# Half a tile of logits, one expert's first products and one addition take other places in a transformer layer's instruction streams

## What is computed

```python
q = einsum(layernorm(x), Wq) / 8;  k = einsum(ctx, Wk);  v = einsum(ctx, Wv)
attn = einsum('bqhd,bkhd->bhqk', q, k)
attn = softmax(einsum('bhqk,hi->biqk', attn, Wth1))
attn = einsum('bhqk,hi->biqk', attn, Wth2)
x = x + einsum(einsum('bhqk,bkhd->bqhd', attn, v), Wo)
feat = layernorm(x).reshape(2048, 256)
scores = layernorm(feat, g, b) @ centroids.T
for e in range(8):            # balanced: each expert takes its 256 best of the rows left
    idx = top_k(where(taken, -inf, scores[:, e]), 256); taken[idx] = True
routed = feat[all idx].reshape(8, 256, 256)
h = gelu(layernorm(routed, g, b) @ w1[e] + b1[e]) @ w2[e] + b2[e]
x = x + (routed + h, put back in row order)
```

## Time and profile before

| | us |
|---|---|
| median of 3 runs | 310.98 (310.86 to 312.36) |
| the profiled execution, its own time | 311.05 |
| span in its profile | 309.3 |
| PE busy in the span | 291.3 |
| DVE busy | 229.2 |
| POOL busy | 198.8 |
| ACT busy | 151.0 |
| device memory read and written | 37.46 MB, mean 121 GB/s |

### The profile page before, as it was taken

One profiled execution on the slowest core, in us unless ns is written; L12 is line 12 of the kernel. 1 busy time (PEld: TensorE's weight loads), 2 busy tenths in 40 slices (PEclk: granted clock), 3 DMA queues, 4 the chain that ended last, 5 costly groups with the idle time before them and its releaser, 6 DMA issues.

```text
span 309.3 us, 6795 instructions
## 1 busy us (share of the span) xinstructions
PE 291.3 (94%) x2151; PEld 252.6 (82%) x2151; DVE 229.2 (74%) x799; ACT 151.0 (49%) x275; POOL 198.8 (64%) x248
## 2 busy tenths in 40 slices
PE   7999998999999999999987779999999999999990
PEld 3989997999999999999982239797989898989980
DVE  0569999888887888888877877777777777338750
ACT  1257646355555555554546424544444454564720
POOL 8200333467888888877742785949787878768841
PEclk9999999999999999999999999999999999999996
DMA  7995002971000000000116420555656565712120
GB/s 254 359 368 207 3 0 76 368 271 35 36 34 34 34 34 34 34 34 35 37 67 206 135 70 2 157 187 166 214 170 208 175 206 174 222 37 69 36 74 28
DMA packets 21769, 37.79 MB, mean 122 GB/s; under 512 B 2416, under 2 KB 14960, under 8 KB 21360
## 3 DMA queue, kind: packets, MB, share of 16 engines
q1 hardware_dynamic: 19184, 31.16, 29.4%
q0 software_dynamic: 2560, 6.31, 6.7%
HBM read 31.17 MB, written 6.29 MB: 121 GB/s over the span
## 4 chain that ended last, share of the span: by engine, by line
PE 77%; DVE 11%; issue 3%; POOL 3%; DMA 2%; ACT 1%; POOLq 0%; DVEq 0%
PE pair L1208 68%; PE pair L1284 4%; PE pair L1258 2%; DVE cmpb L1018 2%; PE pair L1452 1%; PE pair L1296 1%; DMA G<-rows_scratch,idx 1%; DMA out_dram<-G,idx 1%; DVE sm L875 1%; DVE wneg L789 1%; DVE pair L1052 1%; DVE hp L1140 1%; POOL out_dram L543 1%; DVE ok L1035 1%; POOL pr L284 0%
## 5 line engine op out<-in xcount | busy, mean ns | idle before, releaser
L1208 PE MATMUL pair<-yT,w1p 128*128 128x256 f32 x384 | 53.3, 290 | 0.0
L1208 PE MATMUL pair<-Bm,pT 128*128 (+1 forms) x384 | 50.4, 287 | 0.2 <-ACT pT L630 0.2
L1208 PEld LDWEIGHTS pair<-yT,w1p 128*128 128x128 f32 x384 | 48.2, 191 | 0.5 <-POOL yT L528 0.2
L1208 PE MATMUL pair<-Am,xTp 128*128 (+1 forms) x192 | 48.3, 400 | 0.0
L1208 PEld LDWEIGHTS pair<-Bm,pT 128*128 128x128 f32 x384 | 47.1, 191 | 0.4 <-issue 0.4
L1208 PE MATMUL pair<-w2s,hT 128*128 128x256 f32 x192 | 47.1, 389 | 0.0
L284 POOL TENSOR_TENSOR pr<-pr,rs 128x1024 f32<-128x1024 f32 (+1 forms) x16 | 31.3, 1955 | 24.3 <-DVE rs L882 15.2
L522 POOL TENSOR_TENSOR w1p<-w1s,w1p 128x512 fp32r<-128x512 f32 x32 | 40.1, 1280 | 5.7 <-ACT w1p L696 5.6
L1208 PEld LDWEIGHTS pair<-Am,xTp 128*128 128x128 f32 x192 | 34.9, 188 | 6.9
L1208 PEld LDWEIGHTS pair<-w2s,hT 128*128 128x128 f32 x192 | 33.8, 190 | 4.3
L741 ACT ACTIVATE hT<-pair,b1s 128x256 f32<-128x256 f32 x48 | 20.2, 471 | 34.4 <-PE pair L1208 20.9
(11 more groups left out here) (156 smaller groups left out, 573.6 us busy)
## 6 DMA issues: line engine op xcount, KB each, us to landing
w1s<-w_dram SPq DMA_DIRECT2D x8, 1024.0 KB
w2s<-w_dram SPq DMA_DIRECT2D x7, 1024.0 KB, 5.8
rows_scratch<-row SPq DMA_DIRECT2D x16, 256.0 KB, 2.0
xs<-x_dram SPq DMA_DIRECT2D x1, 2048.0 KB, 16.7
xTs<-xT_dram SPq DMA_DIRECT2D x1, 2048.0 KB, 18.4
wk_s<-wk_dram SPq DMA_DIRECT2D x1, 1024.0 KB, 5.5
wv_s<-wv_dram SPq DMA_DIRECT2D x1, 1024.0 KB, 7.6
wqT_s<-wqT_dram SPq DMA_DIRECT2D x2, 512.0 KB, 9.2
```

What stands on the lines that cost most here:

```text
L1208: return nc.tensor.matmul(out_, l, r, start=start, stop=stop)
```

## The change

1. Attention: the statistics of tiles 8 to 15 and their variances leave the fills and come at the end of VectorE's steps 2, 3 and 4; the second root follows in GpSimd's step 5 instead of 0, ACT's wait for it in step 6 instead of 4, and steps 5 and 6 are now written out ahead of the loop. TensorE's step 2 makes the first half (bank) of tile 2's logits ahead of the transposition of tile 0.
2. First expert: in slot 1 its rounded products for f = 0 stand ahead of round 7's total, f = 2's rounded products and the rests of both ahead of the ranks, f = 1 behind the ranks and f = 3 behind the spreading; five filler matmuls go. Slot 2 gets tables of its own for expert 0, with `tokens` and `spread` one piece earlier, and expert 1's first product ahead of the ranks. For all experts ACT's copies come in the order yT(0), yT(1), yF(0), yF(1); the rest of expert 0's second half is made by VectorE ahead of `select(1)`.
3. Last expert: `final(6, 1)` stands ahead of the two `hidden_split` calls of slot 9.

```diff
-        A_FIRST, A_LOOP, A_LOOP_END, A_LAST = -1, 5, 15, T + 4
+        A_FIRST, A_LOOP, A_LOOP_END, A_LAST = -1, 7, 15, T + 4
...
-                if isinstance(s, int) and s in (-1, 0):
-                    x_root(s + 1)
+                if isinstance(s, int) and s in (-1, 5):
+                    x_root(0 if s < 0 else 1)
...
             def y_rest(e, v):
-                for c in range(CC):
-                    pool.wait_ge(e_yT, 4 * e + 2 * c + 2)
+                for c in range(CC if e > 0 else 1):
+                    pool.wait_ge(e_yT, 4 * e + CC + c + 1)
...
-                    if isinstance(s, int) and s in (1, 4):
+                    if isinstance(s, int) and s in (1, 6):
                         act.wait_ge(s_r1, 1 if s == 1 else 2)
...
                 if e > 0:
-                    act.wait_ge(e_yl, CC * e)
+                    act.wait_ge(e_yD, 1)
+                    act.wait_ge(e_yl, CC * e - 1)
...
-                for c in range(CC):
-                    for to in (yF[:, c, :], yT[:, 0, v, c, :]):
-                        nc.scalar.activation(to, bank[0][:, c * CAP:(c + 1) * CAP], ACT.Identity,
+                for to in (yT[:, 0, v], yF):
+                    for c in range(CC):
+                        nc.scalar.activation(to[:, c, :], bank[0][:, c * CAP:(c + 1) * CAP], ACT.Identity,
...
-                if MIXED <= f < MIXED + T // 2:
-                    x_stats(T // 2 + f - MIXED)
-            x_variance(1)
...
+                if isinstance(s, int):
+                    for n in {2: (8, 9), 3: (10, 11, 12), 4: (13, 14, 15)}.get(s, ()):
+                        x_stats(n)
+                    if s == 4:
+                        x_variance(1)
...
+            def first_rows_rest():
+                c = CC - 1
+                dve.wait_ge(e_yT, CC + c + 1)
+                nc.vector.tensor_tensor(yT[:, 1, 0, c, :], yF[:, c, :], yT[:, 0, 0, c, :].bitcast(f32),
+                                        ALU.subtract).then_inc(e_yD, 1)
...
+                    if r == 0 and k - 2 == E - 1:
+                        final(k - 3, 1)
                     if r == 0 and PARTED <= k - 2 < E:
                         hidden_split(k - 2, 2)
                         hidden_split(k - 2, 3)
-                    if r == 2 and 0 <= k - 3 < E:
+                    if r == 2 and 0 <= k - 3 < E and k - 2 != E - 1:
                         final(k - 3, 1)
...
+                if u == 0:
+                    first_rows_rest()
                 if searches(k):
                     select(k)
...
+            def logits(t, v, g):
+                for c in range(CC):
+                    last = mm3(bank[2 * v + g][:], lambda i: xTp[:, i, v, c * P:(c + 1) * P], ...)
+                if g == 1:
+                    last.then_inc(s_lg, 1)
...
             def attn(s, u):
+                ahead = isinstance(s, int) and s == 2
+                if ahead:
+                    pe.wait_ge(s_xTs, s + 1)
+                    pe.wait_ge(s_sub, s - 1)
+                    logits(s, par(s, u, 0), 0)
...
-                    for g in range(2):
-                        for c in range(CC):
-                            last = mm3(...)
-                    last.then_inc(s_lg, 1)
+                    for g in range(1 if ahead else 0, 2):
+                        logits(t, v, g)
...
+            def up_rounded(e, f):
+                if f == 0:
+                    pe.wait_ge(e_w1l, W1_PARTS * (e + 1))
+                up_free(e, f)
+                v, q = e % 2, slice(f * P, (f + 1) * P)
+                for c in range(CC):
+                    pe.wait_ge(e_yT, 4 * e + c + 1)
+                    for i in range(2):
+                        mm(up_bank(f), w1p[:, i, v, c, q], yT[:, 0, v, c, :], c == 0 and i == 0, False)
+
+            def up_rest(e, f):
+                v, q = e % 2, slice(f * P, (f + 1) * P)
+                for c in range(CC):
+                    if e == 0 and c == CC - 1:
+                        pe.wait_ge(e_yD, 1)
+                    elif e == E - 1:
+                        pe.wait_ge(e_yD, 1 + c + 1)
+                    else:
+                        pe.wait_ge(e_yl, CC * e + c + (1 if e == 0 else 0))
+                    mm(up_bank(f), w1p[:, 0, v, c, q], yT[:, 1, v, c, :], False, c == CC - 1)
...
-            UP_FIRST = {2: {8: (0, 1), 9: (1, 2)}, 4: {8: (0, 2), 9: (2, 4)}}
+            UP_FIRST = {4: {8: (0, 2), 9: (2, 4)}}
...
+            UP_REST_0, UP_LATE_1 = {0: (4, 5), 1: (5, 7), 2: (7, 8)}, {8: (0, 1), 9: (1, 2)}
+            DOWN_0 = {2: (0, 2), 3: (2, 5), 4: (5, 8), 5: (8, 10), 6: (10, 12), 7: (12, 15), 8: (15, 16)}
...
+                    rest, downs = (UP_REST[first_part(e)], DOWN[first_part(e)]) if e > 0 else (UP_REST_0, DOWN_0)
+                    for f in range(*rest.get(gap, (0, 0))):
+                        if e == 0:
+                            list_of_tokens(k, gap, 1 - f % 2)
                         up(e, f)
-                        list_of_tokens(k, gap, f % 2)
+                        if e > 0:
+                            list_of_tokens(k, gap, f % 2)
...
-                if 0 <= u < E:
-                    first = UP_LATE if 0 < u < SPLIT else UP_FIRST[first_part(u)]
+                if 0 < u < E:
+                    first = UP_FIRST[4] if u >= SPLIT else UP_LATE if u > 1 else UP_LATE_1
...
                     expert_part(k, r)
+                    if u == 0 and r == 7:
+                        up_rounded(u, 0)
...
-                        keep_busy(1 if k == 1 and r == 0 else BUSY)
+                        keep_busy({(1, 0): 1, (1, 6): 1, (1, 7): 0}.get((k, r), BUSY))
...
                 expert_part(k, 8)
+                if u == 0:
+                    up_rounded(u, 2)
+                    up_rest(u, 0)
+                    up_rest(u, 2)
...
                 expert_part(k, 9)
+                if u == 0:
+                    up(u, 1)
                 if searches(k + 1):
                     if k == 0:
                         keep_busy(2)
                     spread_scores(k + 1)
                     if k == 0:
                         keep_busy()
+                    if u == 0:
+                        up(u, 3)
```

44 lines of the change are left out of this document (18 added, 26 removed).

## The result

The changed kernel takes 309.44 us (median of 9 runs, 309.06 to 309.99). The kernel before, run beside it on the same chip, takes 311.58 (9 runs, 310.86 to 312.95). The ratio is 0.9934, with a 95% interval of 0.9915 to 0.9953: faster by 0.66%, about 2.05 us of 311. The profiled execution took 309.06 us, with a span of 307.2; before it was 311.05 and 309.3. The forecast was 309.3. None of its three terms held its size, and the errors cancel; the rest of the text is about that.

A forecast was written before the change was run, and what follows sets the result against it. TensorE, busy 94% of the span, was taken as the bound except at three touched places where it idles or follows VectorE. 311.05 - 0.9 - 0.4 - 0.4 = 309.35, predicted as 309.3, range 308.5 to 310.7.

The forecast's parts named there:

- Part 1, forecast 0.9: Attention: half of tile 2's logits fills TensorE's 0.91 us idle time before tile 0's transposition; -0.9, moved statistics at 0.
- Filling cannot give more than the gap: TensorE before tile 0's transposition: the gain is at most the 0.91 us idle time.
- The backlog of VectorE: Pipeline rival: moved statistics and root cost tile 4's or 5's cover, giving back 0.5 to 0.9: 309.8 to 310.2; chance 0.13.
- 4.2 in all: VectorE's steps 2 to 4: moved statistics add 0.84, 1.26 and 2.06 us, leaving it at most 1.0 behind at step 5.
- Part 2, forecast 0.4: First expert: slot 1's spreading at its old time, slot 2 shorter with one piece less; -0.4, bounds +0.6 and -0.8.
- the following totals are 0.18 later: Slot 2: gap 2 holds 1.86 us of work against 1.68, so the totals behind it come 0.18 later.
- they are needed only behind the ranks: 0: Other experts: the new order of ACT's copies moves their rests 0.45 later, at a cost of 0.
- Part 3, forecast 0.4: Last expert: the earlier addition shortens TensorE's wait before its last 30 matmuls; -0.4, bounds -0.2 and -0.57.
- the two pairs of splits each end 0.25 to 0.41 later: Last expert: with the addition ahead, the splits end at 297.7 to 297.8, and 27 matmuls start at 297.75 to 297.85.
- The search: Rival in slot 1: subtraction blocked twice or totals late, slot 1 ends 0.4 to 1.0 later: 309.7 to 310.3; chance 0.15.
- The clock: Rival: with five fillers fewer in slot 1 the granted clock falls to 0.50: 312.6 or more, slower; chance 0.04.
- the rival that the parts help each other: Rival set for part 1 alone: gain less than 0.7, kept only if the search's slots are also rearranged; no chance given.

The follow-up runs named there:

- all eight in one step: The changed kernel with all eight moved bn_stats and the variances in VectorE's step 4: 309.63 us, ratio 0.9951.
- the kernel with tokens and addition later: The changed kernel with expert 1's token product one piece later in slot 2 and expert 0's first addition behind the new masked scores: 309.06 us, ratio 0.9936.
- the kernel without fillers: The changed kernel without any filler matmul in slot 1: 311.44 us, ratio 1.0008.
- two variants with the same fillers as the change: The changed kernel with the digit of rounds 0 and 1 through PSUM, 309.85 us, and that with token product and expert 0's addition later too, 309.87.
- attention alone: The kernel before with all edits of part 1 and none of the others: 310.69 us, ratio 0.9981.
- the change without the half tile: The changed kernel without half of tile 2's logits ahead, statistics still in steps 2 to 4: 310.7 us, ratio 0.9979.
- statistics left in place: The changed kernel with statistics, second variances and second root back in their old places, half tile of logits still ahead: 309.66 us, ratio 0.9958.
- both rests on VectorE: The changed kernel with both subtractions of expert 0's rows on VectorE, none on GpSimd: 309.43 us, ratio 0.9946.
- the first rest on GpSimd: The changed kernel with the second subtraction of expert 0's rows back on GpSimd: 310.14 us, ratio 0.9965.
- the first expert alone: The kernel before with all edits of part 2 and none of the others: 311.36 us, ratio 1.001.

## Why the prediction was right, and where its steps were off

The sum was right: 309.3 forecast and 309.44 measured. By the profiles the three parts bring 1.12 + 0.13 + 0.57 = 1.82, where 1.7 was forecast as 0.9 + 0.4 + 0.4. That agreement owes much to luck: parts 1 and 3 gave 0.4 more than forecast and part 2 gave 0.3 less. The level has luck in it as well, as the forecast started from 310.98 and before took 311.58 beside the change; the measured gain is 2.05 us, with an interval of 1.5 to 2.6. The interval's upper end of 0.9953 doesn't quite exclude a gain under the forecast's 0.5%. One sum of the forecast was off: its upper bounds, 0.91, 0.8 and 0.57, add up to 2.3 and not to 2.4 or 2.5.

**Part 1, forecast 0.9, measured 1.12: right mechanism, term too small.** The step that failed is "Filling cannot give more than the gap", with the gap read as the 0.91 of the matmul row. A matmul's row ends later than the next one can start: in the unbroken stream the logits start 0.35 us ahead of the fills' end. Counted by starts, the place lost before was 50.41 - (49.50 - 0.35) = 1.26 us, and the weight loads' row of before says 1.31:

```profile
50.40 0.64 PEld L1284 LDWEIGHTS pair<-cst,pr 128*128 128x128 f32 x6 [1.31 <-DVE Bm L783]
```

The gain of 1.12 lies between the two readings. What it lacks of the 1.26 is the price of the split: from their start to the next product's, the twelve logits took 54.10 - 51.25 = 2.85 us in one piece and (50.65 - 49.08) + (52.91 - 51.44) = 3.04 in two, while the transposition shrank from 0.84 to 0.79; 1.26 - 0.19 + 0.05 = 1.12. The costing of the statistics at nothing held, and the kernels with one half of part 1 each show that it is the half tile alone that pays.

**The backlog of VectorE: right outcome, computed margin much too small.** I left 0.15 us of cover for tile 4's scaling; it is 0.89. The step that failed is "4.2 in all", the moved work with every row's duration charged in full. The sums over the stretches from 50 to 72.2 us, before and then after (us in all; busy us of each engine):

```profile
sum 22.20, PE 21.80 PEld 20.17 DVE 18.86 ACT 10.44 POOL 11.38; mean PE 7.26 PEld 6.72 DVE 6.29 ACT 3.48 POOL 3.79
```

```profile
sum 22.20, PE 22.20 PEld 20.62 DVE 21.99 ACT 11.24 POOL 12.11; mean PE 7.40 PEld 6.87 DVE 7.33 ACT 3.75 POOL 4.04
```

VectorE is busy 21.99 - 18.86 = 3.13 us more, not 4.2: neighbours overlap. The eight bn_stats take 0.74 + 1.07 + 1.07 = 2.88 us in their three rows and not 3.4, and each row begins and ends some 0.08 inside its neighbours. It idled 22.20 - 18.86 = 3.34 there before, near my 1.06 + 2 x 1.05 = 3.16, nearly all of it in waits for TensorE, 0.5 us before a maximum and the rest before its additions (line waited for: us in total, times, longest, before, 50 to 72.3 us):

```profile
DVE x L844 <- PE pair L1208: 2.6, 3, 1.1
```

After, it idles 0.21 us, and the list of its waits in this stretch is empty. So VectorE was late by nothing where I had 1.0, and TensorE's own advance of 1.19 takes the cover of 2.07 down to 0.89. With all eight in one step the scaling came 1.22 later, and the rival came true for the rest, 0.26 to 0.41 us. Its chance of 0.13 was too high for the margin that there was.

**Part 2, forecast 0.4, measured about 0.1: 0.24 in slots 1 to 3, less 0.11 to 0.16 in slot 7.** Slot 1 came out as worked out: ACT's order, the port (0.60 us, 0.28 behind GpSimd), and the masks 1.53 us ahead of the spreading, where 1.48 was assumed. It stands at 185.62 instead of the 185.9 named, mostly because part 1 gave more. In slot 2 the step that failed is "the following totals are 0.18 later". They are 0.24 to 0.31 later, and the kernel with tokens and addition later says why: gap 2's work makes 0.05 to 0.11 of it, and the rest is the token product's earlier place, to which the forecast gave no price. That VectorE's M would then be the bound was right. A second step was missing altogether: slot 3, whose first total is 0.09 later after a spreading that TensorE had to wait for. The kernel with tokens and addition later shows both as causes: it takes 0.35 from slot 2 and gives 0.18 more back in slot 3. The third step that failed is "they are needed only behind the ranks: 0", for the copy order of the other experts. It looked at who reads the rests, and not at what stands behind them on GpSimd: Htk and the last gather, both of which TensorE waits for. The traces show the delay step by step; a kernel with the old copy order for experts 1 to 7 and the rest of the change was not run.

**Part 3, forecast 0.4, measured 0.57.** The step that failed is "the two pairs of splits each end 0.25 to 0.41 later". I took the addition's 0.41 as pushing everything behind it, but before the splits were not limited by VectorE. They came at the pace of ACT and TensorE: two rectified results every 1.44 us (292.27 - 290.83, then 293.71, before as after), and VectorE's two splits of a pair begin 1.32 us after those of the pair ahead when nothing holds them (294.66 - 293.34). The last split ended 297.42 - 294.95 = 2.47 us behind the start of the down products before, and 296.07 - 293.51 = 2.56 after: 0.09 later. TensorE has 21 matmuls to do without it, 21 x 6.07 / 48 = 2.66 us. So the whole wait of 0.57 goes, the bound that I had named as the end of the range. It goes narrowly: the weight loads do wait 0.18 for that split.

**The rivals.** The search did not decide: slot 1 is 0.03 us longer, and the operation was blocked once, by GpSimd's subtraction, not twice. The clock did not fall in the profiled execution of the change: its windows from 174 to 192 us show 1.00 throughout. Two things belong beside that. The mechanism is real and worth 2 us, as the kernel without fillers shows; and two variants with the same fillers as the change had 0.50 for some 3 us in their profiles. The mean clock of those two executions is 0.987, and one of the nine of the change has 0.987 as well, with 309.16 us, faster than most. Five of the 84 executions of before that ran beside the experiments have 0.989 or less, and four of the twelve of attention alone, which has every filler. So such a dip probably happens with and without the five fillers. In which stretch those unprofiled executions had it can't be seen, nor what it costs there: among the low ones are 309.04 us and also 311.95 and 312.54, far above their kernels' medians.

**What the times of the parts say.** Alone they gave 0.43 and 0.49 us faster and 0.24 slower against 311.12, 0.7 in sum, where the whole gave 2.05 against its own runs of before. Attention alone and its complement, the change without the half tile, give 0.43 + 0.42 = 0.85. The intervals are about 0.5 us wide on either side, and the waits in slots 2 and 4 take 0.37 and 0.2 in the profiles of the first two, so a part of the difference is open. The traces speak against the rival that the parts help each other: each place is as long alone as in the whole (13.70, 15.05 and 11.86 us). They put the whole at 1.8, inside its interval, and its nearest relatives in later runs (statistics left in place, all in step 4, both rests on VectorE) came 1.3 to 1.7 us below before.

## What to carry to other kernels

Read an idle gap by the weight loads' row as well as by the matmuls': filling it can give more than the matmuls' row says. Before charging an inserted operation to everything behind it, look at which engine sets the pace there; a chain that follows another engine has spare time in each round, and swallows it. And when work is taken from ahead of one wait, look at what it now stands ahead of: slot 3 paid for slot 2, and only the sum of both slots is the gain. The same holds for an order change on an engine that nobody seems to wait for: follow its instructions on to the next one that somebody needs, here GpSimd's Htk and gather behind the rests, the bias additions and the scatters, and look through every slot for a releaser that wasn't there before.

## What the runs showed of the hardware that was not expected

**A small one-input operation is blocked too.** Line 810, a tensor_scalar of 128x8 on VectorE, took 0.67 us in the change (71.69 to 72.36) while GpSimd's line 440 ran from 71.66 to 72.34, and 0.17 with all statistics in step 4, where GpSimd was idle at that moment; both rows stand above. It took 0.66 to 0.70 in seven further kernels with the same neighbour, and 0.47 in the change without the half tile, where it began 0.23 into the neighbour's row. The same section of the Trainium skill names such operations among those that can contend, and these rows agree; I had counted only the subtraction.

**An unexplained wait on VectorE.** In the kernel with attention alone (timeline of slot 2):

```profile
189.99 0.15 DVE L1042 CAST shi<-acc 128x1 int32<-128x1 f32 x1
190.14 0.98 POOL L512 DMA_INDIRECT G<-rows_scratch,idx  x1 [1.79 <-DVE idx L1125]
...
190.62 0.17 DVE L1055 TENSOR_TENSOR pair<-pair,shi 128x1 int32<-128x1 int32 x1 [0.47 <-DVE shi L1042]
```

In the kernel before, with the same distance of 0.15 between the first two, they stand at 191.52, 191.67 and 191.78, and no wait is shown.

The XOR behind the CAST comes 0.63 us after its start in the one and 0.26 in the other, and the slot is 0.37 us longer. It came 0.62 us after also in the kernel with the first rest on GpSimd, but with the CAST 0.50 behind a gather's issue (191.57 and 191.07) and not 0.15 ahead of one. Waits of 0.24 stand in slot 4 of two others, those with the first expert alone and with the statistics left in place, but there behind the XOR, ahead of the compare. So 4 of the first 10 profiles have a wait near this place, I found no order of the instructions that goes with it, and the try to take it away left the cause open.

**How far the clock's fall reaches.** Without fillers the granted clock stayed at 0.50 for about 10 us, the last 2 of them with TensorE busy all the time; around the fall it had 0.18 us of work in 2. The Trainium skill (TensorE: Matmul & The Clock Gate, Part 1) calls the slow clock the default that activity lifts; the rows agree, and put 2 us on it in this slot.
